# A selective state loop whose states move into two PSUM banks, with its input products on GpSimd

## The reference

```python
dbc = xc @ x_proj_w
delta = jax.nn.softplus(dbc[..., :dt_rank] @ dt_proj_w + dt_proj_b)
Bm = dbc[..., dt_rank:dt_rank + N]
Cm = dbc[..., dt_rank + N:]
A = -jnp.exp(A_log)
deltaA = jnp.exp(delta[..., None] * A)
BX = (delta * xc)[..., None] * Bm[:, :, None, :]
def step(h, inp):
    dA, bx, c = inp
    h = dA * h + bx
    return (h, jnp.einsum('ben,bn->be', h, c))
_, ys = jax.lax.scan(step, h0, (...))
y = jnp.swapaxes(ys, 0, 1) + D_param * xc
y = y * jax.nn.silu(z)
return y @ out_proj_w
```

## Time and profile before

| | |
|---|---|
| median of 3 runs | 2993.48 us (2992.93 to 2994.23) |
| the profiled execution | 2994.06 us |
| its span | 2992.3 us, so 1.76 us lie around it |
| PE, share of the span | 97% |
| DVE | 74% |
| ACT | 56% |
| POOL | 68%, nothing of it in the state loop |
| chain that ended last | PE 92%, DVE 6%, ACT 1% |

### The profile page before, as it was taken

How to read it: one execution, slowest core, us unless ns; L and a number is a source line. 1 busy time by engine, 2 the same in 40 slices (tenths; PEclk the granted TensorE clock), 3 DMA queues, 4 the chain that set the end, 5 groups by cost and what they waited for, 6 DMA issues and landing times.

```text
span 2992.3 us, 41476 instructions
## 1 busy us (share of the span) xinstructions
PE 2901.6 (97%) x14776; PEld 1826.5 (61%) x14776; DVE 2204.6 (74%) x3294; ACT 1673.2 (56%) x2958; POOL 2045.0 (68%) x761
## 2 busy tenths in 40 slices
PE   7999999999999999999999999999999887999999
PEld 4666666666666666666666666666544333445587
DVE  7777777777777777777777777777646899987653
ACT  2567666666767666666666666666623465422021
POOL 1599999999999999999999999999930000002000
PEclk9999999999999999999999999999989988999999
DMA  5544444444445445443444454444350112215100
GB/s 162 143 92 107 103 112 103 100 110 101 111 92 122 99 121 140 110 112 89 115 105 104 100 111 108 92 115 100 70 184 29 42 43 99 85 56 170 71 15 18
DMA packets 145760, 296.26 MB, mean 99 GB/s; under 512 B 36050, under 2 KB 41170, under 8 KB 135986
## 3 DMA queue, kind: packets, MB, share of 16 engines
q1 hardware_dynamic: 135908, 226.76, 27.6%
q0 software_dynamic: 9072, 66.06, 11.8%
q10 hardware_dynamic: 576, 0.79, 0.1%
HBM read 114.47 MB, written 8.06 MB: 41 GB/s over the span
## 4 chain that ended last, share of the span: by engine, by line
PE 92%; DVE 6%; ACT 1%; issue 1%; POOL 0%; DMA 0%; SPq 0%; DVEq 0%; POOLq 0%; ACTq 0%
PE ps L1908 17%; PE ps L1934 16%; PE ps L1947 15%; PE ps L1860 10%; PE ps L1884 9%; PE ps L1891 9%; PE ps L2166 4%; PE ps L2130 3%; PE ps L2146 3%; PE ps L1964 2%; PE ps L1916 1%; DVE bx L1344 1%; DVE pm L1082 1%; PE ps L2158 1%; DVE stats L978 0%
## 5 line engine op out<-in xcount | busy, mean ns | idle before, releaser
L1082 DVE TENSOR_REDUCE pm<-ps 128x1 f32<-128x512 f32 x2048 | 1403.2, 691 | 535.3 <-PE ps L1908 453.6
L1579 ACT ACTIVATE pf<-ps 128x512 f32<-128x512 f32 x2048 | 1203.8, 603 | 654.1 <-PE ps L1934 571.0
L925 POOL TENSOR_TENSOR psum<-psum,pf 128x2048 f32<-128x2048 f32 x317 | 1456.2, 4594 | 18.7
L1908 PE MATMUL ps<-ks,qs 96*128 96x512 f32 x2048 | 832.8, 407 | 8.1 <-DVE pm L1082 3.8
L1934 PE MATMUL ps<-qs,ks 98*128 98x512 f32 x2048 | 814.7, 399 | 1.6 <-ACT pf L1579 1.5
L1908 PEld LDWEIGHTS ps<-ks,qs 96*128 96x128 f32 x2048 | 386.5, 189 | 195.5 <-issue 105.4
L1947 PE MATMUL ps<-pf,V 128*32 128x512 f32 x4096 | 472.5, 602 | 0.0
L1934 PEld LDWEIGHTS ps<-qs,ks 98*128 98x128 f32 x2048 | 391.5, 191 | 46.1 <-ACT pf L1579 12.6
L940 POOL TENSOR_TENSOR ring_r<-ring,w_hi 128x512 fp32r<-128x512 f32 x16 | 21.8, 1373 | 550.7 <-ACT w_hi L1815 550.7
L925 POOL TENSOR_TENSOR psum<-pf 128x2048 f32<-128x2048 f32 x64 | 308.9, 4827 | 50.6 <-ACT pf L1579 50.6
L1884 PE MATMUL ps<-cTh,Wkg 128*128 128x512 f32 x732 | 300.8, 411 | 1.0 <-POOL cTl L889 1.0
(11 more groups left out here) (237 smaller groups left out, 3041.8 us busy)
## 6 DMA issues: line engine op xcount, KB each, us to landing
ks<-KH SPq DMA_DIRECT2D x1024, 64.0 KB, 2.0
psum<-pf POOLq DMA_DIRECT2D x63, 1024.0 KB, 8.6
ks<-KL SPq DMA_DIRECT2D x512, 64.0 KB, 2.0
cT<-in_ctxT SPq DMA_DIRECT2D x32, 768.0 KB, 6.0
Wkg<-wk_rows SPq DMA_DIRECT2D x61, 384.0 KB, 3.0
BC<-bc_rows SPq DMA_DIRECT2D x32, 512.0 KB, 4.8
ring<-in_ffn_w SPq DMA_DIRECT2D x16, 1024.0 KB, 8.1
wA<-in_W_fcT SPq DMA_DIRECT2D x4, 1024.0 KB, 11.4
```

The source lines that it names most:

```text
L925: pool.tensor_tensor(acc, before, pf[:, tile % P_SLOTS, :], ALU.add).then_inc(s_sum, 1)
L1082: dve.tensor_reduce(pm[:, of % 2, n // BLK, n % BLK:n % BLK + 1], src, AX.X, ALU.max).then_inc(s_wfree, 1)
L1579: act.activation(pf[:, tile % P_SLOTS, j * NTOK:(j + 1) * NTOK], ps[:, S_BANK + u % S_BANKS, :], ACT.Exp, scale=SCALE).then_inc(s_exp, 1)
L1908: last = pe.matmul(dst, qs[0:3 * HD, h, t * P:(t + 1) * P], ks[0:3 * HD, keys_of(of, j), i * 512:(i + 1) * 512], start=True, stop=True)
```

## The change

The decays no longer go to SBUF: ACT writes the decay of state s of the pair to PSUM bank 6 + s. DVE scans in place there, and writes the product with C from PSUM to the slot in `bx`. Each of the two states has its own signals. A bank is used again as soon as its product is done, so ACT can be one pair ahead at most, and EXP_LEAD goes from 3 to 1. The input products go to POOL, one instruction per state (`inputs`, now in the gpsimd stream). Since two banks are left for the sums (4 and 5), the pairs go through all states for channel blocks 0 and 1 first, then for 2 and 3 (`state_pair`, EH = 2). The rows of B and C are so loaded twice per batch: 32 loads of 1 MB where there were 16, into four buffers (BC_SLOTS) where there were two, the new ones in the place of `dA`. The gates of blocks 0 and 1 come half-way through a batch.

```diff
-EXP_LEAD = 3
+EH = 2
+EXP_LEAD = 1
+DECAY_BANK = 6
+BC_SLOTS = 4
-GATE_0 = {S_ALL - 1: (0, 1, 2), S_ALL: (3,)}
-GATE_1 = PAIRS - 2
+GATE_0 = {S_ALL // 2: (0,), S_ALL // 2 + 1: (1,), S_ALL - 1: (2,), S_ALL: (3,)}
+GATE_1 = S_ALL + S_ALL // 2
+def state_pair(j):
+    b, i = divmod(j, S_ALL)
+    half, i = divmod(i, EH * S_PER)
+    q, e = divmod(i, EH)
+    return b, q, half * EH + e
...
-    (HIGH, stage(0, "ssm") + stage(1, "ssm") + stage(1, "mix_out") + stage(1, "ln2_T")),
+    (HIGH[:EH], stage(0, "ssm") + stage(1, "ssm")),
+    (HIGH, stage(1, "mix_out") + stage(1, "ln2_T")),
...
 # SP
+                if 2 <= n < BC_SLOTS:
+                    unit_ready(sp, (1, "xw1", F1 // P - 1))
+                elif n >= BC_SLOTS:
+                    sp.wait_ge(s_hc, S_STEP * EH * (n - BC_SLOTS + 1))
...
-            for q in range(2, S_PER):
-                load_bc(0, q)
-                if q == 3:
+            for n in range(S_ALL // EH - 2):
+                load_bc(n)
+                if n == 7:
...
             unit_ready(sp, (1, "dt", KD - 1))
             for n in range(RING):
                 load_piece(n)
-            for q in range(S_PER):
-                load_bc(1, q)
-                if q >= 4:
-                    load_piece(q)
+            for n in range(S_ALL // EH - 2, PAIRS // EH):
+                load_bc(n)
+                if S_ALL // EH + RING + 3 <= n < PAIRS // EH - 1 and n % 2 == 1:
+                    load_piece(RING + (n - S_ALL // EH - RING - 3) // 2)
 # POOL
+            def inputs(j):
+                b, q, e = state_pair(j)
+                n = j // EH
+                if j % EH == 0:
+                    pool.wait_ge(s_bc[n % BC_SLOTS], 32 * (n // BC_SLOTS + 1))
+                if q == 0:
+                    pool.wait_ge(s_delta, b * KD + (e + 1))
+                if j == 2:
+                    pool.wait_ge(s_delta, KD)
+                if j >= S_SLOTS:
+                    pool.wait_ge(s_ysum, j - S_SLOTS + 1)
+                for s in range(S_STEP):
+                    pool.tensor_tensor(bx[:, j % S_SLOTS, s, :], rows_of(n, 0)[:, s, :], dx[b][:, e, :],
+                                       ALU.mult).then_inc(s_bx, 1)
 # DVE
-                dve.wait_ge(s_dA, j + 1)
-                dve.wait_ge(s_bx, j + 1)
                 for s in range(S_STEP):
-                    last = dve.tensor_tensor_scan(bx[:, slot, s, :], dA[:, slot, s, :], bx[:, slot, s, :], 0.0,
-                                                  ALU.mult, ALU.add)
-                last.then_inc(s_scan, 1)
-                if j + 1 < PAIRS:
-                    inputs(j + 1)
-                dve.wait_ge(s_scan, j + 1)
-                dve.tensor_tensor(bx[:, slot, :, :], bx[:, slot, :, :], BC[:, n % 2, 1, :, :],
-                                  ALU.mult).then_inc(s_hc, 1)
+                    state, slot = ps[:, DECAY_BANK + s, :], bx[:, j % S_SLOTS, s, :]
+                    dve.wait_ge(s_dA, S_STEP * j + s + 1)
+                    dve.wait_ge(s_bx, S_STEP * j + s + 1)
+                    dve.tensor_tensor_scan(state, state, slot, 0.0, ALU.mult, ALU.add).then_inc(s_scan, 1)
+                    dve.wait_ge(s_scan, S_STEP * j + s + 1)
+                    dve.tensor_tensor(slot, state, rows_of(j // EH, 1)[:, s, :], ALU.mult).then_inc(s_hc, 1)
 # ACT
-                if j >= S_SLOTS:
-                    act.wait_ge(s_scan, j - S_SLOTS + 1)
                 for s in range(S_STEP):
                     n = S_STEP * q + s
-                    last = act.activation(dA[:, j % S_SLOTS, s, :], delta[b][:, e, :], ACT.Exp,
-                                          scale=negA[:, e, n:n + 1])
-                last.then_inc(s_dA, 1)
-                if j == 1:
-                    hidden(1, range(AHEAD_1, F1 // P))
+                    if j == 0:
+                        unit_emptied(act, LAST_BEFORE[DECAY_BANK + s])
+                    else:
+                        act.wait_ge(s_hc, S_STEP * (j - 1) + s + 1)
+                    act.activation(ps[:, DECAY_BANK + s, :], delta[b][:, e, :], ACT.Exp,
+                                   scale=negA[:, e, n:n + 1]).then_inc(s_dA, 1)
+                if 1 <= j <= 2:
+                    hidden(1, range(AHEAD_1 + 2 * (j - 1), AHEAD_1 + 2 * j))
+                if j == 2:
                     for f in range(KD // 2, KD):
                         gated(0, f)
 # PE, in y_sum
-                pe.wait_ge(s_hc, j + 1)
                 for s in range(S_STEP):
+                    pe.wait_ge(s_hc, S_STEP * j + s + 1)
```

More of the change, by code:

```diff
@@ L243, with last_pair @@
 PER_BATCH = 2 * PIECES_1
+def state_pair(j):
[3 more added lines that the diff above has]
+    return b, q, half * EH + e
+def last_pair(b, e):
+    return b * S_ALL + (e // EH + 1) * EH * S_PER - EH + e % EH
 def stage(b, name):
@@ L259 @@
     (ALL_BANKS, stage(1, "att_T") + stage(0, "xw2")
-     + stage(1, "xw1")[:AHEAD_1] + stage(0, "rms_T") + stage(0, "xz")[:6] + stage(0, "dbc") + stage(0, "dt")
-     + stage(0, "xz")[6:] + stage(1, "xw1")[AHEAD_1:]),
+     + stage(1, "xw1")[:AHEAD_1] + stage(0, "rms_T") + stage(0, "xz")[:6] + stage(0, "dbc") + stage(0, "dt")),
+    (ALL_BANKS[:DECAY_BANK], stage(0, "xz")[6:] + stage(1, "xw1")[AHEAD_1:]),
     (LOW, stage(1, "xw2") + stage(1, "rms_T") + stage(1, "xz")[:KD] + stage(1, "conv") + stage(1, "xz")[KD:KD + 1]
@@ L269 @@
 UNIT_BANK, UNIT_NTH, READY_AT = {}, {}, {}
+LAST_BEFORE = {k: [x for n, x in enumerate(SEGMENTS[2][1]) if n % 8 == k][-1] for k in range(DECAY_BANK, 8)}
 _used, _signalled = [0] * 8, [0] * 8
@@ L374, in emit @@
         s_bcst = sem("s_bcst")
-        s_bc = [sem(f"s_bc{i}") for i in range(2)]
+        s_bc = [sem(f"s_bc{i}") for i in range(BC_SLOTS)]
         s_abs = sem("s_abs")
@@ L487, in emit @@
         xw1 = place("xw1", 96 * K, [P, 2, KD, F1 // 2])
-        dA = place("dA", 96 * K, [P, S_SLOTS, S_STEP, NTOK])
         oin = [place(f"oin{b}", 112 * K + b * (8 * K + 256), [P, NH * NT, HE]) for b in range(NB)]
@@ L491, in emit @@
         above = place("above", 120 * K, [P, KD, NTOK])
-        BC = place("BC", 128 * K, [P, 2, 2, S_STEP, NTOK])
+        BC = [place("BC0", 128 * K, [P, 2, 2, S_STEP, NTOK]), place("BC1", 96 * K, [P, 2, 2, S_STEP, NTOK])]
         w_in = place("w_in", 144 * K, [P, KD, 2 * D])
@@ L527, in emit, with rows_of @@
         lAf_s = place("lAf_s", 202 * K, [P, KD, 3, 2, LR], F32R)
+        def rows_of(n, a):
+            return BC[n % BC_SLOTS // 2][:, n % 2, a, :, :]
         def hid(f):
@@ L780, in store_bc, with load_bc @@
                 sp.wait_ge(s_bcst, b * 16 + 16)
[L782 to L786, removed]
+            def load_bc(n):
+                b, q, _ = state_pair(EH * n)
+                size = S_STEP * NTOK
+                if 2 <= n < BC_SLOTS:
+                    unit_ready(sp, (1, "xw1", F1 // P - 1))
+                elif n >= BC_SLOTS:
+                    sp.wait_ge(s_hc, S_STEP * EH * (n - BC_SLOTS + 1))
                 for a in range(2):
-                    sp.dma_start(BC[:, n % 2, a, :, :].rearrange("p s n -> p (s n)"),
+                    sp.dma_start(rows_of(n, a).rearrange("p s n -> p (s n)"),
                                  bc_rows[b, a, q * size:(q + 1) * size].partition_broadcast(P)
-                                 ).then_inc(s_bc[n % 2], 16)
+                                 ).then_inc(s_bc[n % BC_SLOTS], 16)
             def load_piece(n):
@@ L804, in _ @@
             store_bc(0)
-            for q in range(2):
-                load_bc(0, q)
-            for q in range(2, S_PER):
-                load_bc(0, q)
-                if q == 3:
+            for n in range(S_ALL // EH - 2):
+                load_bc(n)
+                if n == 7:
                     unit_ready(sp, (1, "xw2", NT - 1))
@@ L937, in _ @@
             all_arrived(pool)
+            def inputs(j):
[12 more added lines that the diff above has]
+                                       ALU.mult).then_inc(s_bx, 1)
+            for j in range(PAIRS):
+                inputs(j)
             for m in range(F2 // P):
@@ L1252, in gate @@
                 w = (b, "ssm", e)
-                dve.wait_ge(s_ysum, b * S_ALL + S_ALL - KD + (e + 1))
+                dve.wait_ge(s_ysum, last_pair(b, e) + 1)
                 if e == 0:
@@ L1316, in beside @@
                     second_norm(0, 3)
-                if GATE_1 <= j:
+                if GATE_1 <= j < GATE_1 + EH:
                     gate(1, j - GATE_1)
@@ L2137, in y_sum @@
             def y_sum(j):
-                b, i = divmod(j, S_ALL)
-                q, e = divmod(i, KD)
+                b, q, e = state_pair(j)
                 w = (b, "ssm", e)
```

15 lines of the change are left out of this document (removed).

## The result

The changed kernel takes 3000.82 us (median of 12 runs, 2998.31 to 3003.36), the kernel before on the same chip 2994.10 us (12 runs). The ratio is 1.0025, 95% interval [1.0018, 1.0033]: slower by 6.7 us. The forecast was 3004 us.

A forecast was written before the change was run, and what follows sets the result against it. PE was taken to bound most loop pairs at 5.15 us, DVE 24 others (pairs 0 to 11, 25 to 36). Terms +3.6 and +6.9 gave +10.5 us on 2994.06, so 3004 us; range 2985 to 3014.

The forecast's parts named there:

- likeliest case: The forecast itself, 3004 us at chance 0.45, with its own range of 2997 to 3011 us.
- The sum: Whole kernel: +3.6 us up to pair 11 and +6.9 us in pairs 25 to 36, together +10.5 us.
- 12 collisions: DVE instructions reading two SBUF tensors wait for POOL, 0.96 us each on average; the start's four counted apart.
- (a) Start: Before pair 3: POOL's four instructions alternate with DVE's step-size products, one norm collision; scans of pair 3 +3.8 us.
- (b) Three norm rounds: Three rounds of two pairs and a norm: two collisions each, 15.8 us against 15.47, +0.9 us in all.
- (c) Pairs 9 to 11: End of stretch 1: three savings of 0.8, two collisions (1.9), PE's earlier sum start (-0.6): -1.1 us.
- Pairs 11 to 24: PE-bound pairs stay at 5.15 us; DVE's 3.7 us a pair and ACT's shorter lead are covered.
- Stretch 2: Pairs 25 to 36: POOL waits for late rows of pair 28, deciding by 4.8 us; +6.9 us in all.
- The sign that I named for POOL: At pair 28, POOL's longest wait is one of about 5 to 10 us on the DMA of BC.
- rival 1: DVE and POOL miss each other, so collisions mostly vanish: -6.0 us, 2987.5 us; chance 0.25.
- Rival 2: DVE's 0.8 us a pair comes through, POOL beside scans only, rows of pairs 28 and 29 early: 2983 us; chance 0.12.
- Rival 3: In-place PSUM work costs 0.1 us more for each of 4 instructions in 24 pairs: 9.6 us, 3014 us; chance 0.18.

The follow-up runs named there:

- e9: Kernel before with only the product with C split into two 512-column instructions and PE's sum starting behind the first: 2990.84 us, ratio 0.9995.
- e3: Changed kernel, late rows kept, with PE's sum of a pair waiting for both states again: 3000.33 us, ratio 1.0028.
- e1: Changed kernel with B and C rows of pairs 28 to 31 loaded ahead of the ring of weights: 2993.25 us, ratio 1.0004.
- e2: e1 with POOL's input products held back by waits to fall beside DVE's scans and state products: 2986.32 us, ratio 0.9978.
- e6: e2 with batch 1's step sizes of channel blocks 2 and 3 moved from pairs 32 and 33 to 38 and 39: 2983.32 us, ratio 0.9972.
- e4: Kernel before with only the input products moved to POOL, decays and states left in SBUF: 3013.42 us, ratio 1.0070.
- e8: e1 with POOL waiting for all four step sizes before its first input product: 2993.73 us, ratio 1.0002.
- e7: e6 with ACT's work for batch 1's step sizes spread between single decays from pair 26 on: 2983.49 us, ratio 0.9962.

## Why the prediction was right, and where not

**The direction and the size.** 3000.8 lies in the range and in the likeliest case's own; slower had the greatest chance. The sum was +10.5 us; by mark B it is +7.6, by the median +6.7. The likeliest case's range, 2997 to 3011, is wider than its own bounds give: 12 collisions at 0.5 and at 1.24 us instead of 0.96 make 2998 to 3007, and 3000.8 lies in that too.

**(a) Start, +3.8 forecast.** +3.3: the scan of pair 3 starts at 2351.01 - 2318.85 = 32.2 us against 28.9. All four collisions are there. But in the sum I had put DVE through four whole POOL instructions of 1.24 us, where a collision adds 0.95 or 1.06 us: the scan of pair 0 starts at 9.35 us, not 10.3. The way through ACT and PE to the first norm then took 19.3 us, not 18.2, and the norm's own collision 0.4 us, not 0.96. So part of the agreement is luck.

**(b) Three norm rounds, +0.9.** 16.13, 15.43 and 15.41 us against 15.47: +0.6, with two to three slowed instructions a round, some of them only in part.

**(c) Pairs 9 to 11, -1.1. This is the term that was furthest off.** It came to -3.3 (from +3.9 at the scan of pair 9 to +0.6 at mark A). DVE's part was as sized: from the scan of pair 9 to the end of the product of pair 11 19.84 us instead of 20.36, -0.5. PE's part behind it is 6.52 us instead of 9.27, -2.75, where I had written -0.6. I had given the head start less than half a sum at the upper level of the clock (1.72 / 2 us). But in these pairs PE waits much and its sums run at the lower level, 3.78 us instead of 1.88; then the whole sum stands behind DVE's last product, and starting it one state earlier, and having the level back earlier, is worth most of it. The rows of after, DVE's last product of pair 11 and PE around it:

```profile
2417.13 0.69 DVE L1370 TENSOR_TENSOR bx<-ps,BC 128x512 f32<-128x512 f32 x1
```

```profile
2412.28 7.07 PE L2165 MATMUL ps<-bx,ident 128*128 128x512 f32 x8 [3.71 <-DVE bx L1370]
2419.19 3.60 PE L1880 MATMUL ps<-tT,w_in 128*128 128x512 f32 x8
...
2424.34 3.60 PE L1880 MATMUL ps<-tT,w_in 128*128 128x512 f32 x8
```

e9 shows the effect without PSUM and POOL (-2.9), e3 that the split alone doesn't account for it in the changed kernel (1.1). How much of the rest is the level of the clock is argued from these rows, not shown by a run.

**Pairs 11 to 24.** As forecast: PE is busy 68.00 of 68.00 us in the first stretch of the table above, DVE's saving unseen.

**Stretch 2, +6.9.** +7.0 by the marks, and e1 confirms the cause: the late rows decide, by 6.2 us where I had 4.8. That the sizes agree so well is luck, for errors cancel inside it. The rows landed 1.0 us later than forecast (POOL at 2505.84, 15.8 us behind SP's first issue instead of 14.8), so that from that issue to the scan of pair 32 it was 36.1 us against 27.8, +8.4 and not +7.1. From there to the first feed-forward unit it was 39.8 against 40.9 us, -1.0 and not -0.3; the three collisions forecast for these pairs are in the rows of pair 32, one of them only half (1.15 us), and two waits of 0.2 us for PE's mixing units that DVE had before are gone. The unit itself took 0.3 us less. The sign that I named for POOL, a longest wait of 5 to 10 us on the DMA, was wrong in size: 22.1 us, since POOL had been ahead; the 8.2 us are DVE's wait for POOL.

**The rivals.** The engines don't miss each other (rival 1): POOL starts when `y_sum` frees a slot, which is where DVE does its two-operand work. Rival 2 (2983 us) had the right levers: with its two conditions, rows in time and POOL beside the scans, e2 reaches 2986.3 us, and 2983 took the moved step sizes of e6 as well. Rival 3 is refuted: scans 1.22 us, products 0.69. The Trainium skill (VectorE: DVE Perf Modes, the section on the TRN2 errata) gives a PSUM source 62 cycles more of fixed time; the trace doesn't bear that out, 0.691 us from PSUM against 0.69 from SBUF.

## What to carry to other kernels

When a queue holds two loads and the later one gains a nearer consumer, ask first when it lands: the largest loss here was an order of DMAs that had cost nothing before, and two bounds of a loop undid it. Work moved to GpSimd cost VectorE here about 1 us for each GpSimd instruction that met a VectorE instruction with two SBUF operands; start it from a signal that says VectorE is at work on PSUM. And where PE waits ahead of a long unit, the unit's clock level can give or take 1 to 3 us (3.70 to 6.73 us for the same unit in these kernels), whatever was saved before it; so look at marks on both sides of that unit, and don't credit the difference to the edit.

## What the runs showed of the hardware

- A scan of 512 columns in place in PSUM takes 1.22 us, in SBUF 1.21 us; POOL's products beside it change neither.
- A collision costs DVE 0.95 to 1.06 us (less where the two overlap only in part), and POOL 0.25 to 0.4 us an instruction (1.24 to 1.6), 1.0 us where the two alternate without a break (2.24 in e4). A product of one column costs as much: 1.19 us instead of 0.16.
- Eight matmuls of 512 columns took 3.6 us in steady work, and 3.7 to 6.7 us right behind a gap of 2.3 to 5.2 us in PE's work, by the level of the granted clock. That hid 2.5 of 2.9 us of saved work in e8 and 3.0 of 3.5 in e7; which level a unit gets differs between versions that are otherwise alike.
